# Two graph layers: maxima in one piece, last product by closed blocks, rows fetched on ScalarE's queue

## The reference, cut to what matters

```python
h = relu(layernorm(x)); y = h @ W + b_lin                         # layer 0
logits = leaky_relu(alpha . [y[src], y[dst]])                      # four heads
att = exp(logits - segment_max(logits, dst)); att /= segment_sum(att, dst)[dst]
x = x + segment_sum(att * y[src], dst) + bias
h = relu(layernorm(x))                                             # layer 1
ef = (relu(edge_attr @ We1 + be1) @ We2 + be2) * sigmoid(t * Wt + bt)
msg = relu([h[src], ef] @ Wn1 + bn1) @ Wn2 + bn2
out = x + (segment_sum(msg, dst) + h)
```

## Time and profile before

| | |
|---|---|
| runs, median (lowest to highest) | 2162.62 us (2161.61 to 2163.11), 3 runs |
| profiled execution, its own time | 2157.82 us |
| its span, first to last instruction | 2155.9 us |
| TensorE busy | 1530.4 us (71%) |
| VectorE busy | 1454.3 us (67%) |
| ScalarE busy | 924.3 us (43%) |
| GpSimd busy | 1573.5 us (73%) |
| mean granted TensorE clock | 0.794 |
| DMA packets, bytes | 108,238, 213.36 MB |

### The profile page before, as it was taken

The page is one execution under the profiler, slowest core; times in us unless marked ns, Lnnn a source line. Parts: engine busy times, 40 slices in busy tenths (PEclk is TensorE's granted clock), DMA queues, the critical chain, the costliest instruction groups (busy, mean ns, idle before and its releaser), DMA issues. The chain is left out here.

```text
span 2155.9 us, 42144 instructions
## 1 busy us (share of the span) xinstructions
PE 1530.4 (71%) x8785; PEld 1062.6 (49%) x8785; DVE 1454.3 (67%) x5232; ACT 924.3 (43%) x2807; POOL 1573.5 (73%) x1674
## 2 busy tenths in 40 slices
PE   6555565654555554455658998979988988889986
PEld 4444444433333333334546655646555555555555
DVE  8676676756565565565686886858666666666765
ACT  8535344343352442433476544434443433433431
POOL 7777777777777777777177777777777777777773
PEclk9766665666666676666779998989989899989988
DMA  7222222222222222222164545545555454455443
GB/s 201 55 57 57 56 57 56 57 57 56 56 57 56 56 57 56 56 55 55 25 182 111 149 119 145 148 133 142 143 143 142 137 148 142 113 142 142 122 132 87
DMA packets 108238, 213.36 MB, mean 99 GB/s; under 512 B 33804, under 2 KB 71404, under 8 KB 97999
## 3 DMA queue, kind: packets, MB, share of 16 engines
q0 software_dynamic: 52416, 108.24, 20.6%
q1 hardware_dynamic: 52931, 101.47, 16.8%
q10 hardware_dynamic: 2636, 0.98, 0.2%
HBM read 197.67 MB, written 12.88 MB: 98 GB/s over the span
## 5 line engine op out<-in xcount | busy, mean ns | idle before, releaser
L969 POOL DMA_INDIRECT acc<-table,index x819 | 775.4, 947 | 254.5 <-issue 242.7
L338 POOL DMA_INDIRECT rows<-table,index x771 | 731.5, 949 | 235.0 <-issue 226.8
L481 DVE TENSOR_SCALAR onehot<-iota_row,dst_rel 128x128 f32<-128x128 f32 x832 | 250.2, 302 | 206.4 <-PE pair L649 176.6
L649 PE MATMUL pair<-onehot,rows 128*128 128x128 f32 x1638 | 335.3, 367 | 32.8 <-ACT rows L778 32.8
L778 ACT ACTIVATE rows<-rows,edge_w 128x32 f32<-128x32 f32 x1638 | 352.6, 309 | 2.9 <-issue 1.5
L486 DVE TENSOR_TENSOR acc<-acc,pair 128x256 f32 x832 | 348.7, 419 | 3.1 <-issue 1.7
L649 PEld LDWEIGHTS pair<-onehot,rows 128*128 128x128 f32 x1638 | 287.5, 264 | 101.6 <-ACT rows L778 69.8
L1136 ACT ACTIVATE msg<-pre 128x512 f32<-128x512 f32 x208 | 130.9, 629 | 470.4 <-DVE pre L1266 434.6
L1284 DVE TENSOR_TENSOR acc<-acc,bank 128x128 f32 x832 | 238.6, 287 | 139.0 <-issue 33.2
L1056 PEld LDWEIGHTS bank<-wn1b,ef 128*128 128x128 f32 x1664 | 235.4, 205 | 113.3 <-issue 104.9
L1065 PE MATMUL bank<-onehot,msg 128*128 128x128 f32 x1664 | 236.0, 288 | 59.2 <-ACT msg L1136 59.0
(11 more groups left out here) (162 smaller groups left out, 1201.0 us busy)
## 6 DMA issues: line engine op xcount, KB each, us to landing
ts<-in_ts SPq DMA_DIRECT2D x52, 1024.0 KB
rows_x<-table SPq DMA_DIRECT2D x1664, 0.5 KB
ea<-in_ea_t SPq DMA_DIRECT2D x52, 512.0 KB
rows_y<-table SPq DMA_DIRECT2D x1664, 0.5 KB
acc<-table,index POOLq DMA_INDIRECT x819
rows<-table,index POOLq DMA_INDIRECT x771
table<-feat SPq DMA_DIRECT2D x16, 195.0 KB
table<-x_rows SPq DMA_DIRECT2D x12, 256.0 KB, 2.3
```

Of the source, the lines that this page charges most:

```text
L338: gp.indirect_dma_start(rows0[:, n % (RING * TG), :], None, table1, bass.IndirectOffsetOnAxis(index[:, n:n + 1], 0)).then_inc(half_in[g % ...
L481: dve.tensor_scalar(onehot[:, n // TG % 2, n % TG, :], iota_row[:, :], dst_rel[:, n:n + 1], None, ALU.is_equal).then_inc(oh0, 1)
L649: last = pe.matmul(row_sums[g % 2][:, t * P:(t + 1) * P], row_of(g * TG + t)[:, 0:CH], onehot[:, g % 2, t, :], start=True, stop=True)
L969: gp.indirect_dma_start(rows[:, g % RG1, t, :], None, table, bass.IndirectOffsetOnAxis(index[:, n:n + 1], 0)).then_inc(gathered[g % RG1], 16)
```

## The change

- **Maxima in one piece.** For all turns but the last, `parts_after` gives nothing, and the whole chain of turn r comes behind the last group of turn r - 1 on VectorE and TensorE. For the last turn the pieces come after the fifth to eighth group. `spread_delta` moves behind the first group's small products, `factors` behind the first group's scaling.
- **Rows on ScalarE's queue.** Layer 0: tiles 177, 305, 433, 561, 689 and 817, the second tile of the first group of turns 6, 10, 14, 18, 22 and 26, are fetched row by row, 32 rows (two loads of 16 registers) behind the scaling of each of turns 1 to 24. Layer 1: the first tiles of groups 34, 66, 98, 130, 162 and 194, four rows (one load of 4 registers) behind each of steps 0 to 191. In both, two slots of 128 rows. The addition of such a group's rows in layer 1 is in two instructions, as for SP's tiles.
- **Empty tile.** GpSimd doesn't gather tile 831, and leaves out the 6 tiles of each layer.
- **Last product by closed blocks.** In the last 13 steps of layer 1, from group 195 on, TensorE multiplies by Wn2 the 2 to 4 blocks whose receivers are passed, into the bank of the group's sums, VectorE adds them, and SP writes them out; the separate block at the end is gone.
- Indices for the new rows come by one load in each layer; in layer 0 it goes to the place of the receivers' integers, so SP waits for `rel_done` before it and its own rows. The buffer of the new rows in layer 0 is that of the moments, and `normed1` shares that of `ef`.

```diff
+ACT_BATCH = 16
+ACT_TURNS = 4
+ACT_ROUND = P // ACT_TURNS
+ACT_TILES0 = [SPANS[r][0] * TG + 1 for r in range(ACT_TURNS + 2, TURNS, ACT_TURNS)]
+EMPTY = range(-(-E // P), TILES)
+ENDS = [max(0, N - max(0, E - (g + 1) * GE)) // P if g < GROUPS - 1 else NB for g in range(GROUPS)]
+FIRST_END = next(g for g in range(GROUPS) if ENDS[g] > 0)
+PARTS = GROUPS - FIRST_END
+CUTS = [0] + ENDS[FIRST_END:]
+assert all(0 < y - x <= TG for x, y in zip(CUTS, CUTS[1:]))
+ACT_ROWS = 4
+ACT_STEP = P // ACT_ROWS
+ACT_TILES = [g * TG for g in range(ACT_STEP + 2, GROUPS, ACT_STEP)]
...
-                z = SPANS[r - 1][1]
-                return (3, 4, 5, 6) if r == TURNS - 1 else (z - 3, z - 2, z - 1, z - 1)
+                return (4, 5, 6, 7) if r == TURNS - 1 else ()
...
+                    sp.wait_ge(rel_done, 1)
+                    sp.dma_start(act_index0, a["src_act0"]).then_inc(act_index0_in, 16)
...
@@ -532,16 +550,22 @@
                                 penalties(r)
                             if k == 1:
                                 keep_row_penalties(r)
-                            logits_at, ends_at, carries_at, _ = parts_after(r)
-                            if k == logits_at:
+                            if parts_after(r):
+                                logits_at, ends_at, carries_at, _ = parts_after(r)
+                                if k == logits_at:
+                                    scan_rows(r)
+                                if k == ends_at:
+                                    scan_row_ends(r)
+                                if k == carries_at:
+                                    full_maxima(r)
+                        if r < TURNS:
+                            at = first_of(groups(r)[0])
+                            if not parts_after(r):
                                 scan_rows(r)
-                            if k == ends_at:
                                 scan_row_ends(r)
-                            if k == carries_at:
                                 full_maxima(r)
                         dve.wait_ge(acc0, (span[-1] + 1) * TG)
                         if r < TURNS:
-                            at = first_of(groups(r)[0])
                             rescale(r, at)
                     dve.wait_ge(biased, NB)
...
                         pe.wait_ge(scaled0, (g + 1) * TG * SH)
                         for t in range(TG):
                             last = pe.matmul(row_sums[g % 2][:, t * P:(t + 1) * P], row_of(g * TG + t)[:, 0:CH], onehot[:, g % 2, t, :], start=True, stop=True)
...
                                 continue
                             if k == 0:
                                 turn_penalties(r)
-                            logits_at, ends_at, carries_at, weights_at = parts_after(r)
-                            if k == logits_at:
-                                turn_logits(r)
-                            if k == ends_at:
-                                turn_row_ends(r)
-                            if k == carries_at:
-                                turn_carries(r)
-                            if k == weights_at:
-                                turn_weights(r)
-                                spread_delta(r)
+                            if parts_after(r):
+                                logits_at, ends_at, carries_at, weights_at = parts_after(r)
+                                if k == logits_at:
+                                    turn_logits(r)
+                                if k == ends_at:
+                                    turn_row_ends(r)
+                                if k == carries_at:
+                                    turn_carries(r)
+                                if k == weights_at:
+                                    turn_weights(r)
+                        if r < TURNS and not parts_after(r):
+                            turn_logits(r)
+                            turn_row_ends(r)
+                            turn_carries(r)
+                            turn_weights(r)
...
 
+                    regs = [act.alloc_register(f"line0_{q}") for q in range(ACT_BATCH)]
+
+                    def fetch(r):
+                        j, k = divmod(r - 1, ACT_TURNS)
+                        if r < 1 or j >= len(ACT_TILES0):
+                            return
+                        if r == 1:
+                            act.wait_ge(act_index0_in, 16)
+                            act.wait_ge(table_out, 16 * UNITS_A)
+                        if k == 0 and j >= 2:
+                            act.wait_ge(agg0, ACT_TILES0[j - 2] // TG + 1)
+                        for o in range(k * ACT_ROUND, (k + 1) * ACT_ROUND, ACT_BATCH):
+                            act.load(regs, act_index0[0:1, j * P + o:j * P + o + ACT_BATCH])
+                            for q, v in enumerate(regs):
+                                row = act.snap(v, min_val=0, max_val=N - 1)
+                                act.dma_start(rows_w[o + q:o + q + 1, j % 2, :], table1[ds(row, 1), :]).then_inc(act_row_in[j % 2], 16)
+
                     keep_logits(0)
                     for r in range(TURNS):
                         exponentials(r)
                         keep_weights(r)
-                        factors(r)
-                        if r == 0:
-                            halo(2)
                         act.wait_ge(ew_ready, 2 * (r + 1))
                         for k, g in enumerate(groups(r)):
                             scale_group(r, g)
+                            if k == 0:
+                                factors(r)
+                                if r == 0:
+                                    halo(2)
                             if k == HALF - 1 and r + 3 < TURNS:
                                 halo(r + 3)
                             if r == TURNS - 2 and k == parts_after(r + 1)[0]:
                                 keep_logits(r + 1)
+                        fetch(r)
                         if r < TURNS - 2:
                             keep_logits(r + 1)
...
+                    for i in range(PARTS):
+                        b0, b1 = CUTS[i], CUTS[i + 1]
+                        full = min(b1, N // P)
+                        sp.wait_ge(o_done, i + 1)
+                        sp.dma_start(out[b0 * P:full * P, :].rearrange("(b p) c -> p b c", p=P), x_rows[:, b0:full, :]).then_inc(o_out, 16)
+                        if full < b1:
+                            sp.dma_start(out[full * P:N, :], x_rows[0:N - full * P, full, :]).then_inc(o_out, 16)
+                    sp.wait_ge(o_out, 16 * (PARTS + 1))
 
...
-                            if n not in LINE_TILES1:
+                            if n not in LINE_TILES1 and n not in ACT_TILES and n not in EMPTY:
...
                             pe.wait_ge(acc1, (g - 1) * TG)
+                        if g >= FIRST_END + 2:
+                            pe.wait_ge(o_done, g - FIRST_END - 1)
                         for t in range(TG):
                             last = pe.matmul(bank[6 + g % 2][:, t * P:(t + 1) * P], msg[:, g % 2, t, :], onehot[:, g % 2, t, :], start=True, stop=True)
                         last.then_inc(agg1, 1)
-                    skewed(((0, first_product), (1, second_product), (2, third_product), (3, aggregate)))
+
+                    def last_product(s):
+                        g = s - 4
+                        if g < FIRST_END:
+                            return
+                        pe.wait_ge(acc1, (g + 1) * TG)
+                        for j, b in enumerate(range(CUTS[g - FIRST_END], CUTS[g - FIRST_END + 1])):
+                            last = pe.matmul(bank[6 + g % 2][:, j * P:(j + 1) * P], acc[:, b * P:(b + 1) * P], wn2[:, :], start=True, stop=True)
+                        last.then_inc(f_done, 1)
+                    skewed(((0, first_product), (1, second_product), (2, third_product), (3, aggregate)), last_product)
+                    last_product(GROUPS + 3)
...
+
+                    regs = [act.alloc_register(f"line2_{q}") for q in range(ACT_ROWS)]
+                    act.wait_ge(act_index_in, 16)
+                    for q in range(PROJ_SLOTS):
+                        act.wait_ge(table1_out[q], 16 * len(range(q, UNITS, PROJ_SLOTS)))
+
+                    def fetch(s):
+                        j, o = s // ACT_STEP, s % ACT_STEP * ACT_ROWS
+                        if j >= len(ACT_TILES):
+                            return
+                        if o == 0 and j >= 2:
+                            act.wait_ge(radd, ACT_TILES[j - 2] // TG + 1)
+                        act.load(regs, act_index[0:1, j * P + o:j * P + o + ACT_ROWS])
+                        for q, v in enumerate(regs):
+                            row = act.snap(v, min_val=0, max_val=N - 1)
+                            act.dma_start(rows_z[o + q:o + q + 1, j % 2, :], table2[ds(row, 1), :]).then_inc(act_in[j % 2], 16)
+                    skewed(((0, relu_hidden), (0, time_gate), (2, relu_message)), fetch)
 
...
```

(26 more changed lines are left out.)

74 lines of the change are left out of this document (28 added, 46 removed).

## The result

The changed kernel takes **2124.38 us** (median of 4 runs, 2122.82 to 2125.63) against 2162.86 before: a ratio of 0.9823, 95% interval 0.9809 to 0.9837. Forecast were 2152.5, from 2131 to 2174: right in sign, 28.1 us too high, and outside the range. Its profiled execution took 2122.82 (span 2121.0), 35.0 less than the profiled one before.

A forecast was written before the change was run, and what follows sets the result against it. GpSimd's gathers were to bind layer 1, ScalarE's turn to delay layer 0: +8 layer 0, -8.7 gathers, -12.1 tail, +3 lag make -10 from 2162.6, so 2152.5 us, range 2131 to 2174.

The forecast's parts named there:

- the sum for ScalarE's turn: Layer 0: scaling and halo 14.0, factor wait 0.95, rows 16.2, chain 6.6: 37.7 us a turn against 39.0 of gathers.
- The price of the rows: ScalarE's queue, layer 0: 32 rows a turn at SP's 0.505 us a row, 16.2 us.
- the extra copies: Layer 0, turns with a tile fetched by ScalarE: an extra copy moves turn 25's scaling from 1030.5 to 1033.
- start of layer 1: End of layer 0: about 8 us later, though its gathers end 8.7 us earlier.
- Rival 1: Layer 0: gathers still bind if ScalarE's turn is 36.9 us or less; total 2132 us; chance 0.25.
- The lag: Last 13 groups of layer 1: added products and additions fill TensorE and VectorE, costing 3 us (0 to 8).
- The tail: Behind the last additions: 7.9 us to the end of the span instead of 20.0, a gain of 12.1.
- The gathers of layer 1: Layer 1: seven gathers left out at 1.25 us each, 8.75 us gained, as gathers bind there.
- The latency of the chain in one piece: Layer 0, copy of the logits to scaling: 6.6 us instead of 12.93.
- The short load in layer 1: ScalarE's queue, layer 1: each load of 4 registers takes 0.75 us, between 0.3 and 1.23.
- Rivals 2 and 3: ScalarE's turn costs more and binds layer 0, up to 2205, chance 0.22; SP binds layer 1, over 10 us, 0.08.
- Rival 3's sign: Layer 1: TensorE's waits for edge attributes would grow through the layer if SP became the bound.

The follow-up runs named there:

- e6: The changed kernel, with ScalarE's queue waiting for its own last scaling before it issues each turn's rows in layer 0: 2122.70 us.
- e16: The kernel before with the last product by closed blocks alone (new index loads stayed): 13.1 us (7 to 19) under the kernel before.
- e17: The changed kernel with GpSimd gathering ScalarE's six tiles of layer 0 again: about 5.8 us slower against its own before, span 4.1 us longer.
- e9: The changed kernel with ScalarE waiting for its last scaling before the rows, and its layer 0 register loads bringing 4 indices instead of 16: 2217.24 us.

## Why the prediction was wrong

- **The failed step** is the sum for ScalarE's turn, 14.0 + 0.95 + 16.2 + 6.6 = 37.7, with its premise "VectorE is not in it: its sums of a turn end about ... 28 us after the scaling starts, ScalarE asks for the chain at 31". It takes the turn as one line of work. The price of the rows was right (from the first load at 137.9 to 140.32 + 13.69 = 154.0, 16.1 us), but 2.4 us of it lay under the last scalings, since ScalarE's queue issues while its engine still works. ScalarE asks at 28.3, VectorE is free at 29.4, and the chain takes 6.3 from there: 35.7.
- **What of it moved the total** is shown by e6: without the overlap the turn is 36.96 us, and the total is the same. So even as one line of work the sum was 0.8 us too high. The scaling with its waits takes 14.54 us (14.95 taken), the rows 16.2, copy to scaling 6.13 (6.6 taken). The prediction's own terms of the chain, with the 0.8 us of hops, add up to 7.2 and not to the 6.4 that it gives. Over 24 turns the error is 17 us (1030.5 - 1013.3); the extra copies, 2.5 us, don't show, as e6's average turn is as long as its first. So turn 25 starts near 1013 and not at 1033. A further 1.3 us lie between it and layer 1 (77.0 us, 79.3 before, about 78.3 forecast). All this is 21.7 of the 28.1 us (start of layer 1: +8 predicted, -13.7 measured).
- **The point between the bounds,** 36.94, decides the case. Rival 1 had it ("36.9 us or less"), named the cause of the short turn in part ("because the sequencer runs ahead"), and got a chance of 0.25. The forecast lay 0.8 us beyond that point, as much as its sum was wrong.
- **The lag** of the last groups was 0.9 us (1.4 in e16), 3 taken. Its premise, one group's 4.99 us of gathers against 4.95 of TensorE, was right in kind: from 2074 to 2098, with products and additions running, a step took 4.78 us.
- **The tail** behind the last additions gave 15.0 us instead of 12.1; with the lag that is 14.1 instead of 9.1. Wrong were the three last products, 0.94 us for 1.5 (the granted clock was 1.00 there, the upper level, after TensorE had multiplied until 2115.24, 0.85 us before), and the stretch from the last output's issue to the end, 2.9 for 4.65.
- **The gathers of layer 1** gave 7.1 of 8.75. In e17, with the same 812 gathers, it is 8.1, and 819 gathers took 1024.7 to 1025.7 us in three traces, so much of this is noise. They ran back to back all the same: TensorE's waits for edge attributes total 42.4 us in the changed kernel and 40.0 before (row below), the last of 0.9 us at 1711.8, and cost the gathers nothing that the trace shows. In layer 0 the seven gathers gave 7.0 us.

```profile
L1041 PE MATMUL pair<-ea,we 64*128 64x512 f32 x416 | 248.2, 678 | 40.0 <-DMA ea<-in_ea_t 40.0
```

- **The executions:** the median of before stood 4.8 us above its profiled one, that of after 1.6. That is 3.2 of the 28.1. With the 5.0 us of tail and lag they are why the result lies below the range too, whose foot was rival 1's 2132: its time was 7.6 us too high, though its mechanism held.
- **Right:** the price of 32 rows. The latency of the chain in one piece within 0.4 us, 6.6 taken, 6.2 measured (1006.32 to 1012.53), which times 24 is not small. The short load in layer 1, 0.486 us for 0.75 taken, hidden anyway. The Trainium skill, DMA: Bandwidth & Descriptors, section "Latency and other measured facts", gives such a load a floor of about 600 ns; the 192 loads of layer 1 (row below) lie below it, the median of e9's, 588 ns, at it:

```profile
L1236 ACTq TENSOR_LOAD <-act_index x192: 481/486/565, 1141.0 to 2025.8; - x192
```

- **Rivals 2 and 3** fell. With SP issuing beside it, ScalarE's rows have a median of 234 ns and SP's 225, as before, and SP's 1664 rows of layer 0 take 838.8 us from first to last, 838.6 before. Rival 3's sign is there in small: TensorE's waits for edge attributes total 42.4 to 55.1 us in the eight traces with ScalarE's rows in layer 1, 33.9 to 45.1 in the four without (those with a kernel before of 2160 us). The gathers ran on beside these waits, and what lengthens them was not tried. The lock that the Trainium skill describes (Perfetto Trace Analysis, section "DMA Instruction — HWDGE (DVE, Sync)") cost the rows of either queue nothing that their medians show:

```profile
L826 ACTq TENSOR_LOAD <-dst_int x48: 1187/1252/1447, 137.9 to 993.6; - x48
...
L308 SPq DMA_DIRECT2D rows_x<-table x1664: 224/225/318, 83.1 to 921.9; - x185
...
L829 ACTq DMA_DIRECT2D moments<-table x768: 234/234/552, 139.3 to 1001.6; - x192
```

## What to carry to other kernels

For a loop shared by several engines, write down when each engine is ready for the next turn, and price an addition by what it adds to the latest of them, not to its own queue's sum. If the forecast stands within an error or two of the point where the bound changes hands, give both sides their chance and both times. To lengthen a queue for a test, use work whose result is read, and count the instructions in the trace before reading the time.

## What was not expected of the hardware

- Loads of registers are not linear in their size. On ScalarE's queue in layer 0, 16 took 1252 ns, 4 took 588 and 2 took 776 (medians); in layer 1, 4 took 486, so the number of registers isn't all that counts. With the loads of 2 alone the median issue of a row rose too, from 234 to 356 ns.
- The same program took 2160 us beside some runs and 3232 to 3313 beside others, with the durations of gathers and of the largest groups on VectorE and ScalarE within 4%, and SP's rows 1.08 us apart in a stretch of layer 1 where they are otherwise 0.45 apart. There the tail by closed blocks costs 0.5 to 0.7%, and the changed kernel without its rows in layer 0 is 3.7 to 3.8% slower than the kernel before. What sets one or the other is open.
